# Gated linear attention with a depthwise convolution on 8 cores: two convolution taps per product on shifted copies of 64 channels, in two column tiles

## The chip, the cores and the metric

The kernel runs on all 8 cores of one Trainium2 chip, one launch for all. Each batch (4 of them) belongs to two cores: the even core computes the first 2560 tokens of the 4096, the odd core runs the state over these (without any output) and computes the other 1536. The metric is the device time of the slowest core, in microseconds. Names of engines: TensorE is PE, VectorE is DVE, ScalarE is ACT, GpSimd is POOL, SyncE is SP (here it only issues DMAs and waits).

## The reference

For each batch of 4096 tokens with 1024 features:

- layer norm, then `mixed = x W_qkv^T` (3072 channels), a causal depthwise convolution over time with 4 taps for each channel, and silu: `c[ch, t] = silu(sum over k of w[ch, k] * mixed[ch, t - 3 + k])`. The result is split into q, k and v with 16 heads of 64.
- `z = x W_z^T`, a gate `beta = sigmoid(x W_b^T)` and a decay `g = -exp(A_log) * softplus(x W_a^T + dt_bias)` for each head and token.
- q and k are normalised over the head; the state `S = S * exp(g) + k (beta v)^T` runs over the tokens, `o = q S`.
- `o` is normalised over the head, multiplied by silu(z), multiplied by W_out and added to x.
- layer norm, a product with a 1024 x 1024 matrix that is unfolded from small tensor-train factors, plus bias, added to the input of this norm.

## The kernel before, in words

**Tiles and steps.** Tokens go in tiles of 512 (`TT`), and a tile in four chunks of 128 (`NCH`). Channels go in blocks of 128 (`cc`): 0 to 7 are q, 8 to 15 k, 16 to 23 v, 24 to 31 z. An even core has 5 own tiles (`NPRE` 0, `NOWN` 5), an odd core 5 tiles that it only runs the state over (`NPRE` 5; 16 blocks, k and v, with 4 in each step) and 3 own tiles (24 blocks with convolution and 8 of z; the steps have 7, 7, 7 and 3 blocks, and the last one the z blocks too). The main loop (L1050) is software pipelined: in one step, attention works on chunk `g` of tile `t`, projection and convolution on a part of tile `t + 1`, the output product on chunk `n - 1` and the last product (`ffn`) on chunk `n - 2`. The order of instructions on every engine is the order in which this program issues them; `Lane.need` puts a wait in front, `Lane.mark` an increment behind, and every engine runs its own queue in order.

**Projection (`proj`, L508).** A block is 8 products of 128 x 128 weights and 128 x 512 columns (`proj_mm`, L503) into one of three PSUM banks (`pR`, given in turn by `ring`, L456, which waits for the release of the bank). The result is moved to `pre[:, j, 3:515]` as bf16, behind three columns that the tile before left (`halo_in` and `halo_out`, L474 and L484): by DVE for even `j` (L530), by ACT for odd `j` (L527). All blocks of a step are projected first (`fe`), then all are convolved (`fc`), with pieces of the attention between.

**Convolution (`conv`, L545).** Four products (L550), one for each tap: the stationary operand is a diagonal 128 x 128 matrix with that tap's weights, the moving operand is `pre[:, j, tap:tap + 512]`. Silu on ACT moves the sum out (L556). For k, ACT squares it too (L563), and `k2_flush` sums the squares by small products.

**Diagonal blocks (`d_issue`, L375).** In the first use of a block DVE builds the four diagonals (L386) from an identity and the taps, `d_keep` (L392) stores them in DRAM (`dscr`), and every later use loads them from there (L383). Both DMAs go through the SP queue, whose order is: wait, issue, wait, issue; a store of `dscr` in this queue waits for the build, a load waits for the convolution that frees its buffer and for the store. `ND` = 6 buffers are in turn, so a block is asked for six convolutions ahead. Weights of the projection go the same way: first use by a casting DMA from the input on the POOL queue (L366), a store to `wscr` (L373) and later loads (L363) on the SP queue.

**Attention.** `tvk` transposes v and k (TensorE) and scales them (DVE, L723 and L728); `decay` gives the decay matrix (TensorE, exp on ACT L752, cut to the triangle by POOL L756); `qk` multiplies scores by it (DVE L777); `oT` (L794) gives the output chunk in products of 64 columns with `tile_position` (0, 64 par) (L807) and (64 par, 64 par) (L813); `state` updates the state; `gate_out`, `outproj` and `ffn` follow in later steps. The norms are DVE instructions (L431, L935) and their transposes are DMAs on the SP queue (L449, L939). POOL also does q squared (L791), the bias (L945), the state's decay (L839) and its cast (L875).

**Unfolding.** In the first tiles, DVE builds the matrix of the last product in 72 pieces, some behind every projection (`uf`, L1003; 3 pieces on even cores, 1 on odd ones).

Of the kernel before, what the change touches and what calls it, by code (L numbers as in the profile page):

```python
# [5 lines left out]
F32 = mybir.dt.float32  # L6
# [9 lines left out]
NW, ND, NP, NK = 5, 6, 7, 4  # L16


def host_prep(inputs):
# [14 lines left out]
    cw = np.ascontiguousarray(  # L34
        conv_w[:, 0, :].reshape(24, 128, 4).transpose(1, 0, 2).reshape(128, 96))
# [36 lines left out]
    def t2(G2):  # L72
# [76 lines left out]
def build_program():  # L149
# [30 lines left out]
    dscr = dint("dscr", [24, 128, 512], BF16)  # L180
# [21 lines left out]
    ln2 = sb("s_ln2", [128, D])  # L202
    ln2T = [sb(f"s_ln2T{i}", [128, 8, 128]) for i in range(2)]
# [34 lines left out]
    i128b = sb("s_i128b", [128, 128])  # L238
    biasb = sb("s_biasb", [128, 1024])
# [41 lines left out]
    def emit(NPRE, NOWN):
# [44 lines left out]
        t_wab, t_i128f, t_cw, t_prow, t_bones32, t_i128b = (q_c[i].tok for i in range(6))  # L326
# [891 lines left out]
```

How the kernel before makes its waits and increments, by code:

```python
    def mark(self, ins):  # L110
        ins.then_inc(self.h, 1)
        self.v += 1
        return (self, self.v)
# [1 line left out]
    def need(self, *toks):  # L115
        for tok in toks:
            if tok is None:
                continue
            src, val = tok
            if val <= 0 or self.seen.get(src.name, 0) >= val:
                continue
            self.e.wait_ge(src.h, val)
            self.seen[src.name] = val
# [10 lines left out]
    def go(self, lane, out, in_):  # L134
        lane.e.dma_start(out=out, in_=in_).then_inc(self.h, 16)
        self.v += 16
        return (self, self.v)
# [1 line left out]
    def gotr(self, lane, out, in_):  # L139
        lane.e.dma_start_transpose(out=out, in_=in_).then_inc(self.h, 16)
        self.v += 16
        return (self, self.v)
# [122 lines left out]
    def begin(eng, name, out, in_):  # L265
        eng.dma_start(out=out, in_=in_).then_inc(sem(name), 16)
        begun.add(name)
```

## Time and profile before

| | us |
|---|---|
| median of three runs (lowest, highest) | 892.13 (885.72, 893.48) |
| the profiled execution | 892.11 |
| its span, first to last instruction of the slowest core (core 2) | 890.2 |
| spans of the eight cores | 879.7 to 890.2 |

| engine, core 2 | busy us | share of the span |
|---|---|---|
| TensorE, products | 686.3 | 77% |
| DVE | 487.2 | 55% |
| ACT | 296.8 | 33% |
| POOL | 266.9 | 30% |

The profile is one execution. Even cores and odd cores run different programs, and the slowest of all sets the time, so both kinds are to be read. A share of busy time is an average over parts with different bounds. Ends of products are modelled, so that the pitch from start to start is the safer measure of TensorE. Where a line says "x8", it is a run of instructions merged in order of time.

### The profile page before, as it was taken

The numbers are of one execution on the slowest core, as the hardware profiler recorded it, in microseconds if no ns is written. First come the engines' busy times: TensorE is split into PE (matmuls) and PEld (weight loads), VectorE is DVE, ScalarE is ACT, GpSimd is POOL, SyncE is SP. The second block draws the span as 40 slices with busy tenths as digits, with TensorE's granted clock in tenths as the row PEclk, the third lists the DMA queues.
The fourth block names the chain that finished last, engine by engine and source line by source line (L and its number), as shares of the span: only waits on it lengthen the run. The fifth ranks groups of instructions, "written<-read, shape, count | busy, mean of one in ns | idle before, by whom it ended". The sixth has DMA issues, their size and how long they took to land.

```text
span 890.2 us, 14242 instructions; the slowest of 8 cores (879.7 to 890.2 us)
## 1 busy us (share of the span) xinstructions
PE 686.3 (77%) x4687; PEld 316.4 (36%) x4767; DVE 487.2 (55%) x678; ACT 296.8 (33%) x522; POOL 266.9 (30%) x317
## 2 busy tenths in 40 slices
PE   0768674689887979979897997897999897665543
PEld 0323231234343424434343443443444443332211
DVE  4537784245656365666546657633465453656532
ACT  1143340246434325433434444413543343111100
POOL 2122111033324150450514315325044152334410
PEclk9998896799998989999899999989999999766668
DMA  9598986876366663744746456365374464122222
GB/s 195 118 238 168 182 198 184 200 205 188 78 181 171 156 175 100 203 129 152 193 132 193 122 176 168 105 169 136 116 190 105 106 163 109 41 77 67 84 59 63
DMA packets 102223, 129.00 MB, mean 145 GB/s; under 512 B 48382, under 2 KB 65284, under 8 KB 102016
## 3 DMA queue, kind: packets, MB, share of 16 engines
q1 hardware_dynamic: 88272, 99.38, 39.2%
q0 software_dynamic: 13872, 28.63, 16.7%
q8 instruction: 42, 0.69, 0.3%
q14 instruction: 37, 0.30, 0.1%
HBM read 107.40 MB, written 22.76 MB: 146 GB/s over the span
## 4 chain that ended last, share of the span: by engine, by line
PE 53%; DMA 20%; DVE 11%; issue 7%; ACT 4%; SPq 2%; POOL 2%; DVEq 0%; ACTq 0%; POOLq 0%
PE pR L503 20%; PE pR L550 9%; PE pB L912 9%; PE pA L953 7%; DMA dscr<-s_d 6%; DMA s_w<-wscr 5%; DMA wscr<-s_w 3%; DMA s_rb<-rscr 3%; DVE s_ln L935 2%; SPq L140 1%; DMA s_i128b<-i 1%; PE pB L807 1%; DMA rscr<-s_r 1%; PE pB L813 1%; DVE s_ktil L728 1%
## 5 line engine op out<-in xcount | busy, mean ns | idle before, releaser
L503 PE MATMUL pR<-s_lnxT,s_w 128*128 128x512 bf16 x1240 | 314.7, 405 | 73.2 <-DMA s_w<-wscr 27.3
L503 PEld LDWEIGHTS pR<-s_lnxT,s_w 128*128 128x128 bf16 x1280 | 126.9, 102 | 239.7 <-issue 115.7
L550 PE MATMUL pR<-s_pre,s_d 128*128 128x512 bf16 x460 | 117.1, 386 | 15.7 <-DVE s_pre L530 9.3
L135 POOL DMA_DIRECT2D rscr<-s_r x40 | 22.2, 558 | 267.4 <-ACT s_r L884 92.1
L912 PE MATMUL pB<-s_wout,s_gated 128*128 128x512 bf16 x308 | 80.7, 416 | 23.5 <-DVE s_og L826 11.6
L556 ACT ACTIVATE s_post<-pR 128x512 bf16<-128x512 f32 x120 | 68.9, 593 | 64.1 <-PE pR L550 63.6
L530 DVE CAST s_pre<-pR 128x512 bf16<-128x512 f32 x70 | 48.0, 688 | 70.1 <-PE pR L503 70.1
L918 DVE TENSOR_TENSOR s_x<-pB,s_x 128x1024 f32<-128x1024 f32 x20 | 24.5, 1225 | 101.2 <-PE pB L912 101.2
L953 PE MATMUL pA<-s_wbig,s_ln2T 128*128 128x512 bf16 x312 | 73.2, 384 | 6.6 <-DMA s_ln2T<-s_ln 6.1
L550 PEld LDWEIGHTS pR<-s_pre,s_d 128*128 128x128 bf16 x480 | 41.6, 98 | 64.5 <-issue 19.7
L527 ACT CAST s_pre<-pR 128x512 bf16<-128x512 f32 x50 | 29.3, 585 | 96.2 <-PE pR L503 96.1
L573 ACT ACTIVATE s_zT<-pR 128x512 bf16<-128x512 f32 x40 | 23.7, 597 | 110.2 <-PE pR L503 100.3
L912 PEld LDWEIGHTS pB<-s_wout,s_gated 128*128 128x128 bf16 x320 | 33.2, 106 | 66.9 <-issue 36.8
L875 POOL CAST s_Sb<-s_S 128x512 bf16<-128x512 f32 x20 | 12.2, 608 | 146.3 <-DVE s_ssb L870 146.3
L556 ACT ACT_TABLE_LOAD x20 | 25.7, 1283 | 77.6 <-PE pR L550 77.6
L756 POOL TENSOR_SCALAR_AFFINE_SELECT s_dsb<-s_dsb 128x1024 bf16<-128x1024 bf16 x40 | 44.4, 1110 | 23.6 <-ACT s_dsb L752 23.1
L414 ACT ACT_TABLE_LOAD x21 | 26.9, 1283 | 71.1 <-DVE s_pre L480 58.5
L135 POOL DMA_DIRECT2D s_w<-wcat x31 | 17.2, 557 | 101.0 <-DMA wscr<-s_w 38.8
L953 PEld LDWEIGHTS pA<-s_wbig,s_ln2T 128*128 128x128 bf16 x320 | 31.3, 99 | 44.6 <-issue 8.3
L958 DVE TENSOR_TENSOR s_x<-pA,s_x 128x1024 f32<-128x1024 f32 x20 | 24.5, 1225 | 41.1 <-PE pA L953 41.1
L945 POOL TENSOR_TENSOR s_x<-s_x,s_biasb 128x1024 f32<-128x1024 f32 x20 | 42.6, 2129 | 14.2 <-DVE s_ln L935 14.2
L897 DVE TENSOR_TENSOR s_gated<-s_og,s_rb 128x1024 bf16<-128x1024 bf16 x20 | 25.0, 1250 | 29.5 <-DMA s_rb<-rscr 29.5
(118 smaller groups left out, 891.7 us busy)
## 6 DMA issues: line engine op xcount, KB each, us to landing
s_w<-wscr SPq DMA_DIRECT2D x128, 256.0 KB, 4.6
s_d<-dscr SPq DMA_DIRECT2D x96, 128.0 KB, 3.4
s_x<-x SPq DMA_DIRECT2D x22, 512.0 KB, 5.7
s_rb<-rscr POOLq DMA_DIRECT2D x40, 256.0 KB, 4.7
y<-s_x SPq DMA_DIRECT2D x20, 512.0 KB, 2.9
s_xa<-x SPq DMA_DIRECT2D x18, 512.0 KB, 6.4
s_w<-wcat POOLq DMA_DIRECT2D x32, 256.0 KB, 6.2
wscr<-s_w SPq DMA_DIRECT2D x32, 256.0 KB, 5.6
```

Of the source, the lines that this page charges most:

```text
L135: lane.e.dma_start(out=out, in_=in_).then_inc(self.h, 16)
L414: t = S.mark(S.e.activation(out=bn[:, 14:15], in_=bn[:, 13:14], func=AF.Ln, bias=EPS5))
L503: ins = P.e.matmul(ps, w[:, dc * 128:(dc + 1) * 128], lnxT[u % 2][:, dc, :], start=(dc == 0), stop=(dc == 7))
L527: te = S.mark(S.e.copy(out=pre[:, j, 3:515], in_=ps))
L530: te = V.mark(V.e.tensor_copy(out=pre[:, j, 3:515], in_=ps))
L550: ins = P.e.matmul(ps, dr[i % ND][:, tap * 128:(tap + 1) * 128], pre[:, j, tap:tap + 512], start=(tap == 0), stop=(tap == 3))
L556: silu_tok[(u, cc)] = ring_free[k] = S.mark(S.e.activation(out=post[u % 2][:, cc, :], in_=ps, func=AF.Silu))
L756: exp_tok[(n, h2)] = G.mark(G.e.affine_select(out=d3, in_=d3, pattern=[[0, 8], [1, 128]], compare_op=ALU.is_ge, fill=zero_reg, base=0, cha ...
L897: gat_tok[n] = V.mark(V.e.tensor_tensor(out=gated.rearrange("p (a b) -> p a b", a=8), in0=og.rearrange("p (a b) -> p a b", a=8), in1=rb, o ...
L912: ins = P.e.matmul(pB[:, hf * 512:(hf + 1) * 512], gated[:, cc * 128:(cc + 1) * 128], wout[:, cc, hf * 512:(hf + 1) * 512], start=(cc == 0 ...
L945: xb_tok[n] = G.mark(G.e.tensor_tensor(out=x2[n % 3], in0=x2[n % 3], in1=biasb, op=ALU.add))
L953: ins = P.e.matmul(pA[:, hf * 512:(hf + 1) * 512], ln2T[n % 2][:, dg, :], wbig[:, dg, hf * 512:(hf + 1) * 512], start=(dg == 0), stop=(dg ...
```

## The change

The 128 channels of a block are treated as two strips of 64. `pre` gets two strips for each block: partitions 0 to 63 hold the strip's projection as before (columns 3 to 514 behind the halo), partitions 64 to 127 hold the same 64 channels shifted by one column (4 to 515). A product then has 128 rows of contraction and gives two taps at once: the stationary operand is 128 x 64, two diagonals of 64 one above the other. A block takes two passes for each of two strips, so four products of 64 columns; strip 0 goes to columns 0 to 63 of the array and PSUM partitions 0 to 63, strip 1 to columns 64 to 127 and PSUM partitions 64 to 127, in alternation.

The evacuation of a projected block is four instructions instead of one: ACT copies PSUM partitions 0 to 63 twice (to both halves of strip 0), DVE copies PSUM partitions 64 to 127 to the shifted half of strip 1 and then, inside SBUF, that to its unshifted half. The bank is free after ACT's second and DVE's first copy; the convolution waits for ACT's second and DVE's second. The halo is copied by two instructions each way.

The diagonal blocks (128 x 4 x 64) are built by GpSimd for every use, seven convolutions ahead; `dscr`, its stores and its loads are gone. To make room, the second norm shares its buffer with the first (`ln_buf`), `ln2T` has one buffer instead of two, and the squares of k have three instead of four.

The diff, cut to its core:

```diff
-NW, ND, NP, NK = 5, 6, 7, 4
+NW, ND, NP, NK = 5, 7, 7, 3
...
-    cw = np.ascontiguousarray(
-        conv_w[:, 0, :].reshape(24, 128, 4).transpose(1, 0, 2).reshape(128, 96))
+    taps = conv_w[:, 0, :].reshape(24, 2, 64, 4)
+    cw = np.zeros((128, 24, 2, 2), np.float32)
+    for ps_ in range(2):
+        cw[0:64, :, :, ps_] = taps[:, :, :, 3 - 2 * ps_].transpose(2, 0, 1)
+        cw[64:128, :, :, ps_] = taps[:, :, :, 2 - 2 * ps_].transpose(2, 0, 1)
...
-    dr = [sb(f"s_d{i}", [128, 512]) for i in range(ND)]
+    dr = [sb(f"s_d{i}", [128, 4, 64]) for i in range(ND)]
-    pre = sb("s_pre", [128, NP, 516])
-    halo = sb("s_halo", [128, 24, 4])
+    pre = sb("s_pre", [128, NP, 2, 516])
+    halo = sb("s_halo", [128, 24, 2, 4])
-    ln2 = sb("s_ln2", [128, D])
-    ln2T = [sb(f"s_ln2T{i}", [128, 8, 128]) for i in range(2)]
+    ln2T = sb("s_ln2T", [128, 8, 128])
...
         def d_issue(i):
...
-            if cc in dscr_tok:
-                Y.need(prev, q_ds[sl].tok, dscr_tok[cc])
-                d_tok[i] = q_d[sl].go(Y, dr[sl], dscr[cc])
-            else:
-                V.need(prev, q_ds[sl].tok, t_i128f, t_cw)
-                d_tok[i] = V.mark(V.e.tensor_tensor(
-                    out=dr[sl].rearrange("p (a b) -> p a b", a=4),
-                    in0=i128f[:, None, :].broadcast_to([128, 4, 128]),
-                    in1=cw[:, cc, :, None].broadcast_to([128, 4, 128]), op=ALU.mult))
-                dscr_tok[cc] = None
+            G.need(conv_tok[d_uses[i - ND]] if i >= ND else None, t_i64f, t_cw)
+            d_tok[i] = G.mark(G.e.tensor_tensor(
+                out=dr[i % ND], in0=i64f[:, None, :].broadcast_to([128, 4, 64]),
+                in1=cw[:, cc, :, None].broadcast_to([128, 4, 64]), op=ALU.mult))
...
         def halo_in(u, E):
...
-                halo_tok[u] = V.mark(V.e.tensor_copy(out=pre[:, 0:k, 0:3],
-                                                     in_=halo[:, p0:p0 + k, 0:3]))
+                V.e.tensor_copy(out=pre[0:64, 0:k, :, 0:3], in_=halo[0:64, p0:p0 + k, :, 0:3])
+                halo_tok[u] = V.mark(V.e.tensor_copy(
+                    out=pre[64:128, 0:k, :, 1:4], in_=halo[64:128, p0:p0 + k, :, 0:3]))
...
         def proj(u, cc, j):
...
-            if j % 2 == 1:
-                S.need(t, conv_tok[old] if old else None)
-                te = S.mark(S.e.copy(out=pre[:, j, 3:515], in_=ps))
-            else:
-                V.need(t)
-                te = V.mark(V.e.tensor_copy(out=pre[:, j, 3:515], in_=ps))
-            ring_free[k] = evac_tok[(u, cc)] = te
+            S.need(t, conv_tok[old] if old else None)
+            S.e.copy(out=pre[0:64, j, 0, 3:515], in_=ps[0:64, :])
+            ts = S.mark(S.e.copy(out=pre[64:128, j, 0, 4:516], in_=ps[0:64, :]))
+            V.need(t)
+            t1_ = V.mark(V.e.tensor_copy(out=pre[64:128, j, 1, 4:516], in_=ps[64:128, :]))
+            V.need(t1_)
+            tv_ = V.mark(V.e.tensor_copy(out=pre[0:64, j, 1, 3:515],
+                                         in_=pre[64:128, j, 1, 4:516]))
+            ring_free[k] = [ts, t1_]
+            evac_tok[(u, cc)] = (ts, tv_)
...
         def conv(u, cc, j):
...
-            P.need(evac_tok[(u, cc)], halo_tok[u], d_tok[i])
+            P.need(*evac_tok[(u, cc)], halo_tok[u], d_tok[i])
             k, ps = ring()
-            for tap in range(4):
-                ins = P.e.matmul(ps, dr[i % ND][:, tap * 128:(tap + 1) * 128],
-                                 pre[:, j, tap:tap + 512], start=(tap == 0), stop=(tap == 3))
+            for ps_ in range(2):
+                for st in range(2):
+                    off = 3 - 2 * ps_
+                    ins = P.e.matmul(ps[64 * st:64 * st + 64, :], dr[i % ND][:, 2 * st + ps_, :],
+                                     pre[:, j, st, off:off + 512], start=(ps_ == 0),
+                                     stop=(ps_ == 1), tile_position=(0, 64 * st))
             t = conv_tok[(u, cc)] = P.mark(ins)
-            d_keep(i)
             d_issue(i + ND)
...
         def ln2_norm(n):
             bn = bnB[n % 2]
-            V.need(l2rs_tok[n], l2_tok.get(n - 1))
+            lk = ln_buf()
+            V.need(l2rs_tok[n], ln_user[lk])
...
-            Y.need(t, ffn_tok.get(n - 2))
-            l2_tok[n] = q_tr2[n % 2].gotr(Y, ln2T[n % 2], ln2)
+            Y.need(t, ffn_tok.get(n - 1))
+            l2_tok[n] = ln_user[lk] = q_tr[lk].gotr(Y, ln2T, lnx[lk])
```

## Rows read from the trace of the kernel before

**Rows 1.** The cores, each with its span and its mean granted TensorE clock.

```profile
core 2: 890.2 us, clock 0.908
core 5: 887.3 us, clock 0.901
```

**Rows 2.** Busy us (x instructions) by engine, granted clock, DMA share, GB/s, core 2, by stretch.

```profile
27.00:167.00 140.00, 93.59 (x415) 37.22 (x419) 80.98 (x151) 40.87 (x70) 24.31 (x44) 0.88 0.83 181
167.00:747.00 580.00, 513.29 (x3683) 239.85 (x3750) 324.95 (x427) 231.93 (x403) 187.47 (x210) 0.96 0.56 152
```

**Rows 3.** Groups by shape, core 2: xcount, busy us, mean ns, idle before with its releasers.

```profile
L550 PE MATMUL pR<-s_pre,s_d 128*128 128x512 bf16 x460 | 117.1, 386 | 15.7 <-DVE s_pre L530 9.3 <-DVE s_d L386 3.2 <-issue 2.5
L530 DVE CAST s_pre<-pR 128x512 bf16<-128x512 f32 x70 | 48.0, 688 | 70.1 <-PE pR L503 70.1
L527 ACT CAST s_pre<-pR 128x512 bf16<-128x512 f32 x50 | 29.3, 585 | 96.2 <-PE pR L503 96.1
L386 DVE TENSOR_TENSOR s_d<-s_i128f,s_cw 128x512 bf16<-128x512 f32 x24 | 15.4, 687 | 20.8 <-DMA dscr<-s_d 20.7
L990 DVE CAST s_wbig<-s_x 128x512 bf16<-128x512 f32 x4 | 1.7, 427 | 0.4
```

**Rows 4.** Timeline of core 2, first tile: start us, us, engine, line, what [idle before].

```profile
94.00 0.69 DVE L386 TENSOR_TENSOR s_d<-s_i128f,s_cw 128x512 bf16<-128x512 f32 x1 [4.03 <-DMA dscr<-s_d]
96.97 3.57 PE L503 MATMUL pR<-s_lnxT,s_w 128*128 128x512 bf16 x8 [4.87 <-DVE s_pre L530]
...
148.45 0.53 POOL L135 DMA_DIRECT2D s_w<-wcat  x1 [17.73 <-DMA wscr<-s_w]
```

**Rows 5.** Timeline of core 2, attention products and convolution in a step.

```profile
368.02 0.41 PE L807 MATMUL pB<-s_dsb,s_vtok 128*64 128x128 bf16 x8
368.36 0.41 PE L813 MATMUL pB<-s_eb,s_Sb 64*64 64x128 bf16 x8
371.25 1.91 PE L550 MATMUL pR<-s_pre,s_d 128*128 128x512 bf16 x8
```

**Rows 6.** Busy time of the second step of an own tile, core 2.

```profile
350.20:380.80 30.60, 30.07 (x226) 14.46 (x229) 21.45 (x26) 13.17 (x23) 10.72 (x11) 1.00 0.64 178
```

**Rows 7.** Timeline of core 2, a first step and a second step of a tile.

```profile
327.19 3.57 PE L503 MATMUL pR<-s_lnxT,s_w 128*128 128x512 bf16 x8 [3.77 <-DMA s_w<-wscr]
...
357.99 3.61 DVE L431 TENSOR_SCALAR s_lnx<-s_xa,s_bnA 128x1024 bf16<-128x1024 f32 x1
358.07 1.11 POOL L756 TENSOR_SCALAR_AFFINE_SELECT s_dsb<-s_dsb 128x1024 bf16<-128x1024 bf16 x1
359.14 1.90 POOL L791 TENSOR_TENSOR s_qsq<-s_post 128x1024 bf16<-128x1024 bf16 x1
362.24 1.11 POOL L756 TENSOR_SCALAR_AFFINE_SELECT s_dsb<-s_dsb 128x1024 bf16<-128x1024 bf16 x1
363.31 2.13 POOL L945 TENSOR_TENSOR s_x<-s_x,s_biasb 128x1024 f32<-128x1024 f32 x1
365.40 1.04 POOL L839 TENSOR_TENSOR s_S<-s_S,s_gam 128x512 f32<-128x512 f32 x1
367.52 1.21 DVE L777 TENSOR_TENSOR s_dsb<-pA,s_dsb 128x1024 bf16<-128x1024 f32 x1
```

**Rows 8.** Single lines, core 2: min/median/max ns, first and last start, forms.

```profile
L486 DVE COPY s_halo<-s_pre x20: 167/180/2930, 46.4 to 719.0; 128x21 bf16<-128x21 bf16 x15, 128x9 bf16<-128x9 bf16 x5
L431 DVE TENSOR_SCALAR s_lnx<-s_xa,s_bnA x18: 791/1926/4245, 8.8 to 575.4; 128x1024 bf16<-128x1024 f32 x18
L788 DVE TENSOR_TENSOR s_eb<-s_post,s_eb x20: 678/684/2376, 176.0 to 829.2; 128x1024 bf16<-128x1024 bf16 x20
```

**Rows 9.** Busy time by stretch, core 1 (odd): one tile of 16 blocks, then 350 to 480.

```profile
229.90:284.00 54.10, 49.39 (x360) 24.03 (x355) 37.35 (x69) 31.92 (x53) 5.22 (x6) 1.00 0.73 189
350.00:480.00 130.00, 102.97 (x652) 46.26 (x651) 50.29 (x91) 46.03 (x77) 25.42 (x37) 0.91 0.70 164
```

**Rows 10.** Timeline of core 1 where a tile begins.

```profile
229.33 0.63 PE L587 MATMUL pG<-s_lnxT,s_wab 128*32 128x128 bf16 x32 [0.66 <-DMA s_lnxT<-s_lnx]
```

More of the change, by code:

```diff
@@ L81, in host_prep @@
         i128=np.eye(128, dtype=np.float32),
+        i64=np.tile(np.eye(64, dtype=np.float32), (2, 1)),
         ind48=np.tile(ind16, (3, 1)),
@@ L325, in emit @@
             xa_tok[m] = q_xa[m].tok
-        t_wab, t_i128f, t_cw, t_prow, t_bones32, t_i128b = (q_c[i].tok for i in range(6))
+        (t_wab, t_i128f, t_cw, t_prow, t_bones32, t_i128b,
+         t_i64f) = (q_c[i].tok for i in range(7))
         t_sel = cload(Y, sel, d_sel)
@@ L429, in ln1_norm @@
             bn = bnA[m % 2]
-            V.need(rs_tok[m], tr_tok.get(m - 2))
+            lk = ln_buf()
+            V.need(rs_tok[m], ln_user[lk])
             norm_tok[m] = V.mark(V.e.tensor_scalar(
-                out=lnx[m % 2], in0=xbuf(m), scalar1=bn[:, 12:13], scalar2=bn[:, 15:16],
+                out=lnx[lk], in0=xbuf(m), scalar1=bn[:, 12:13], scalar2=bn[:, 15:16],
                 op0=ALU.subtract, op1=ALU.mult))
@@ L479, in halo_in @@
                 V.need(halo_saved[0])
-                halo_tok[u] = V.mark(V.e.tensor_copy(out=pre[:, 0:k, 0:3],
-                                                     in_=halo[:, p0:p0 + k, 0:3]))
+                V.e.tensor_copy(out=pre[0:64, 0:k, :, 0:3], in_=halo[0:64, p0:p0 + k, :, 0:3])
+                halo_tok[u] = V.mark(V.e.tensor_copy(
+                    out=pre[64:128, 0:k, :, 1:4], in_=halo[64:128, p0:p0 + k, :, 0:3]))
         def halo_out(u, E):
             p0, k = spos(u, E[0]), len(E)
-            V.need(*[evac_tok[(u, cc)] for cc in E[-2:]], halo_tok[u])
-            halo_saved[0] = V.mark(V.e.tensor_copy(out=halo[:, p0:p0 + k, 0:3],
-                                                   in_=pre[:, 0:k, 512:515]))
+            V.need(*[x for cc in E for x in evac_tok[(u, cc)]], halo_tok[u])
+            V.e.tensor_copy(out=halo[0:64, p0:p0 + k, :, 0:3], in_=pre[0:64, 0:k, :, 512:515])
+            halo_saved[0] = V.mark(V.e.tensor_copy(
+                out=halo[64:128, p0:p0 + k, :, 0:3], in_=pre[64:128, 0:k, :, 513:516]))
         silu_tok, ksq_tok, k2_tok, z_tok = {}, {}, {}, {}
@@ L516, in proj @@
                 V.need(P.mark(ins))
-                ring_free[k] = halo_tok[u] = V.mark(V.e.tensor_copy(out=pre[:, j, 0:3],
-                                                                   in_=ps[:, 1:4]))
+                for st in range(2):
+                    r_ = slice(64 * st, 64 * st + 64)
+                    V.e.tensor_copy(out=pre[0:64, j, st, 0:3], in_=ps[r_, 1:4])
+                    halo_tok[u] = V.mark(V.e.tensor_copy(out=pre[64:128, j, st, 1:4],
+                                                         in_=ps[r_, 1:4]))
+                ring_free[k] = [halo_tok[u]]
             i, k, ps, t = proj_mm(u, cc)
@@ L572, in zproj @@
             S.need(t, og_tok.get(4 * (u - 1 - NPRE) + 3))
-            z_tok[(u, cc)] = ring_free[k] = S.mark(S.e.activation(
-                out=zT[:, cc - 24, :], in_=ps, func=AF.Silu))
+            z_tok[(u, cc)] = S.mark(S.e.activation(out=zT[:, cc - 24, :], in_=ps, func=AF.Silu))
+            ring_free[k] = [z_tok[(u, cc)]]
         gtok = {}
@@ L933, in ln2_norm @@
             bn = bnB[n % 2]
-            V.need(l2rs_tok[n], l2_tok.get(n - 1))
+            lk = ln_buf()
+            V.need(l2rs_tok[n], ln_user[lk])
             t = norm2_tok[n] = V.mark(V.e.tensor_scalar(
-                out=ln2, in0=x2[n % 3], scalar1=bn[:, 12:13], scalar2=bn[:, 15:16],
+                out=lnx[lk], in0=x2[n % 3], scalar1=bn[:, 12:13], scalar2=bn[:, 15:16],
                 op0=ALU.subtract, op1=ALU.mult))
-            Y.need(t, ffn_tok.get(n - 2))
-            l2_tok[n] = q_tr2[n % 2].gotr(Y, ln2T[n % 2], ln2)
+            Y.need(t, ffn_tok.get(n - 1))
+            l2_tok[n] = ln_user[lk] = q_tr[lk].gotr(Y, ln2T, lnx[lk])
         xb_tok = {}
@@ L952, in ffn @@
                 for hf in range(2):
-                    ins = P.e.matmul(pA[:, hf * 512:(hf + 1) * 512], ln2T[n % 2][:, dg, :],
+                    ins = P.e.matmul(pA[:, hf * 512:(hf + 1) * 512], ln2T[:, dg, :],
                                      wbig[:, dg, hf * 512:(hf + 1) * 512],
@@ L1181, in emit @@
                         out=lhalo, in_=lnxT[(NPRE - 1) % 2][:, :, 508:512]))
-        for q in (q_w + q_wc + q_ws + q_d + q_ds + q_xa + q_x2 + q_tr + q_tr2 + q_y + q_c + q_b3 + q_eb
+        for q in (q_w + q_wc + q_ws + q_xa + q_x2 + q_tr + q_y + q_c + q_b3 + q_eb
                   + q_rb + q_e + q_r + [q_a, q_i]):
```

41 lines of the change are left out of this document (23 added, 18 removed).

## The prediction, made before the change was run

> **What bounds the kernel now.** I read the spans of the cores first, then the busy time by stage, then the groups by shape, then the timelines of a few stretches. The slowest core is core 2, one of the even ones; the slowest odd core, core 5, ends 2.9 us earlier [rows 1]. Even cores run five tiles with all 24 channel blocks each, odd ones five tiles with 16 and three with 24, so both kinds have to be worked out. On core 2 the span has three parts: the first tile (27 to 167 us), with TensorE busy 94 of 140 us and the DMA engines 83%; four tiles in which attention and projections interleave (167 to 747 us), with TensorE busy 513 of 580 us [rows 2]; and the 143 us behind, a tail without convolutions. TensorE bounds the middle; DVE is at 56% there. The tail keeps its work and its waits.
>
> **The change part by part.**
>
> Products. A block has four convolution products of 512 columns. Eight of them take 1.91 us, one alone 0.386, so the pitch is (1.91 - 0.386)/7 = 0.218 us [rows 3, 5] and a block costs 0.87 us. Now there are again four, each on 64 columns of the array, in alternating column tiles. The attention has products of that form: eight with 128 moving columns start and are followed by the next kind 0.34 us later, 43 ns each with one change of tile form in it [rows 5], while 218/4 = 54 ns would be needed one after another. So the two column tiles overlap, and I price a block at half, 0.44 us. The other end is no overlap, 0.87 us. Saved on TensorE: 0.44 x 24 = 10.5 us in each full tile, 52 us on core 2. Eight overlapping at 27 ns would take 0.22 us, so a change of form costs at most 0.13 us; a step of an own tile gets about one more (outproj and ffn are now neighbours of another form, oT and state of the same): 16 x 0.13 = 2 us, which I leave in the error.
>
> Evacuation. Before, a block was moved out of PSUM by one instruction, DVE at 0.688 us (70 times) or ACT at 0.585 us (50 times) [rows 3]. Now each block takes two ACT copies (1.17 us) and on DVE one PSUM copy (0.688) and one copy SBUF to SBUF that waits for it. The trace has no bf16 copy of this size; the nearest is the 512-element cast inside SBUF at 0.427 us [rows 3], which I take as 0.43; the ends are 0.17 us (a 21-element copy, [rows 8]) and 0.69 us. ACT: 190 more at 0.585 = 111 us on top of 297, less than half the span. DVE: 120 x 1.12 = 134 us instead of 48.0. So DVE gets 86 us more here and loses 15.4 with the diagonal blocks [rows 3]. In the middle stage it goes from 325 to 325 + 96 x 1.12 - 56 x 0.69 = 394 of 580 us. That is not a bound by the share, but it sits in the projection phase of a step.
>
> Diagonal blocks. Off DVE: 24 builds. On GpSimd: 120 builds of 256 elements; an f32 product of 512 elements takes 1.04 there [rows 7], so 0.5 to 1.04 us, I take 0.55: 66 us on 267. Each waits for a convolution on TensorE and is made seven blocks ahead, a whole step, so no convolution waits for it. Queued behind it on GpSimd are the next build, the state's cast and DMA issues for the next step; none is wanted before that step, so I price it at nothing; without this cover it would be 0.55 us a block. Off the SP queue go 96 loads and 24 stores with their waits. Sharing the norm buffers, the single ln2T and three ksq buffers cost nothing: what they wait for ended one step before, or one product before the ACT instruction in front.
>
> First tile. DVE waited 20.8 us in front of its builds, nearly all for the store of an earlier one [rows 3]. One case: the build of 94.00 came 4.03 us late, the evacuation behind it too, and TensorE stood 4.87 us [rows 4]. Later the stores of weights stood behind diagonal traffic on SP, and GpSimd waited 17.73 us for one before it could ask for the next weights [rows 4]. DVE loses 15.4 + 20.8 = 36 us and gets 24 x 1.12 - 14 x 0.69 = 17 us: 19 less. The DMA engines lose 24 stores and 7 loads of 0.13 MB, 4.1 MB of 181 GB/s x 140 us = 25 MB: 22 us if they bound alone. DVE (19) and DMA (22) are both near; I take 17, and 5 to 28 as ends. A weight takes its time however early it is asked for.
>
> The step of an own tile, in which the gain is at stake. Take the second step of a tile, 30.6 us long [rows 6], and count from its start at 350.2. DVE has by then the sums and statistics of the step before to do and is free at about 2.9. Before, DVE ended the second product of scores and decay (L777) at 368.73, so at 18.5 [rows 7]; the attention's oT waits for it. Now DVE has before that point: halo 0.65, seven blocks at 1.12 (7.8), vtok and ktil 2.4 (of L777's length, 1.2), two norms at 0.8 and qtil at 0.68 [rows 8], two score products 2.4 = 15.5, so it ends at 18.4, as before. The three convolutions in front of oT gain nothing; the four behind it gain 4 x 0.44 = 1.8 us.
>
> But DVE doesn't get through undisturbed. A norm of 0.8 us took 3.61 us, from 357.99 to 361.60, while GpSimd ran from 358.07 to 361.04 without a gap [rows 7]; the 21-element copy inside SBUF took up to 2.93 us against 0.17, and the norm of the first line has a median of 1.93 against 0.79 [rows 8]. The f32 and bf16 copies out of PSUM show nothing of this. The Trainium skill, SBUF — State Buffer, section "Who interferes with whom", says why: GpSimd and a DVE copy or tensor_scalar in a two-port mode exclude each other for a whole instruction. The trace agrees by the two cases above. The new copy is one inside SBUF like L486, seven times a step. In this step GpSimd has stretches of 3.0 us (358.07 to 361.04) and 4.2 us (362.24 to 366.44) [rows 7]. The first held a norm already and will hold a copy in its place, with the norm still to come; I take 2.5 us. The second held nothing large; it comes about 1.5 us later, because ACT reaches the decay's exponentials behind more copies, and then holds the norm for most of its length, 3.4 us. DVE ends L777 at 18.4 + 5.9 = 24.3, and with the 1.8 us behind it the step is 4.1 us longer. In the first and third steps TensorE waits for a weight load (3.77 us, [rows 7]) whose issue on SP stands behind a norm. This wait covers the same delay, so there the seven blocks give 7 x 0.44 = 3.1 us back; in the third the gates' work comes in front of the norm and takes, as I estimate, 1.9 of it: -3.1 and -1.2. The last step has three blocks and eight z, whose products cover little: one held copy, +1. Tile: -3.1 + 4.1 - 1.2 + 1 = +0.8, times four = +3. Ends: -8 a tile (nearly all of 10.5 reaches the end) and +14 (three steps like the second).
>
> Odd cores. In the tiles with 16 blocks DVE is busy 37.35 of 54.1 us [rows 9]; 16 x 1.12 - 8 x 0.69 = 12.4 more makes 49.8, so the saved product time (16 x 0.44 = 7) finds DVE in the way. At the end of a tile TensorE already waits 0.66 us for the transposed norm [rows 10], which stands behind the blocks on DVE, now about 2 us later. I add 4 us for each of four tiles, +16 (0 to 30). The first tile gains 15, the tile in which the q and z weights come first (350 to 480 us, TensorE busy 103 of 130, [rows 9]) gains 12, for the same stores. The two tiles after that: +1.
>
> Sum. Even: 890.2 - 17 + 3 = 876. Odd: 887.3 - 15 - 12 + 16 + 1 = 877. The profiled execution took 892.11 us for its span of 890.2, 1.9 more, and the median of the runs is 892.13, so no correction: 878 and 879, and the slowest of eight a little above: **880 us**.
>
> **The rivals.**
> - GpSimd decides (slower). If a GpSimd stretch holds DVE in the second step's way in the first three steps of each own tile, it costs 12 x 4.1 = 49, plus 4 for the last steps, less 17: 892 + 36 = 928; halfway to the forecast, 904. It decides where the held DVE time exceeds TensorE's wait for weights, 3.8 us a step. For it: [rows 7, 8]. Against: where TensorE waits anyway it costs nothing.
> - The whole gain arrives (faster). DVE and ACT keep up, 8 us a tile and 20 at the start: 892 - 32 - 20 = 840. For it: DVE at 56%. Against: the sum of DVE's list up to L777.
> - The products don't overlap: the change does not do what it says. TensorE saves nothing, DVE's list remains, the start gains 10 less: 892 - 7 + 4 x 3 = 897, with 3 a tile for the held copies that no shorter product pays for. Against: 43 ns [rows 5].
>
> **How the numbers follow.** Forecast 0.45, its own range 865 to 895; GpSimd 0.27; whole gain 0.18; no overlap 0.10. The range reaches to 855 and to 915, which leaves out about two thirds of the whole gain's case and a third of GpSimd's, 0.2 together. A measurement of this kernel can tell about 1% (8.9 us) from no change: faster means below 883. Forecast gives 0.27 faster, 0.14 same, 0.04 slower; GpSimd 0.04 same, 0.23 slower; whole gain 0.18 faster; no overlap 0.07 same, 0.03 slower. Sum: 0.45, 0.25, 0.30.
>
> **What would show it.** The convolution's products at a pitch of about 0.11 us (half of 0.218); the SBUF copy at 0.43 us alone and at 2 us and more beside GpSimd; DVE busy near 560 us on core 2; the first tile ended near 150 instead of 167; the interval of four own tiles near 580 us still, with TensorE's idle time in front of L777's reader up. The forecast is wrong if the SBUF copy is never held, or held at each step, or if the first tile stays at 167.

## The result, and the profile after

The changed kernel takes 935.33 us (median of 4 runs, 932.31 to 938.81), beside it the kernel before 888.92: ratio 1.052, 95% interval 1.045 to 1.060. It is slower by 46 us; 880 was forecast. The profiled execution took 932.31 us. All spans grew, those of the odd cores most: to 913.6 to 918.0 us on even cores, 918.7 to 930.7 on odd ones. (Some executions of a program on eight cores are disturbed; the ratios leave these out, and where too few are left none is given.) TensorE's granted clock fell from about 0.91 to 0.86 (compare [rows 1]).

```profile
core 2: 913.6 us, clock 0.873
core 5: 930.7 us, clock 0.855
```

Both kernels compute the gates with TensorE once at the start of every tile (L587 before, L606 after). From start to start, in us, the last interval to the end of the span:

| | first starts | tiles |
|---|---|---|
| core 2 before | 26.9 | 140.1, 141.1, 149.7, 146.8, 285.7 |
| core 2 after | 30.2 | 126.5, 144.6, 157.0, 157.0, 298.4 |
| core 5 before | 33.9 | 84.6, 57.0, 53.6, 61.1, 56.1, 120.7, 135.0, 285.4 |
| core 5 after | 32.7 | 74.3, 66.9, 65.6, 78.5, 65.8, 114.3, 136.2, 296.4 |

The first tile is shorter on both, as forecast. On core 2 every tile behind it is longer; on core 5 it is the four tiles of 16 blocks behind the first (+49) and the last own one. The tail is not: from the start of its last projections to the end core 2 has 148.9 us before, 149.8 after.

Groups by shape on core 2 after, columns as in [rows 3]:

```profile
L544 DVE COPY s_pre<-s_pre 64x512 bf16<-64x512 bf16 x120 | 90.4, 754 | 12.7 <-DVE s_pre L542 0.5
L568 PE MATMUL pR<-s_pre,s_d 128*64 128x512 bf16 x480 | 82.8, 445 | 37.0 <-DVE s_pre L542 21.7 <-DVE s_pre L544 8.5 <-DVE s_wbig L1016 4.4
L388 POOL TENSOR_TENSOR s_d<-s_i64f,s_cw 128x256 bf16<-128x256 f32 x120 | 75.7, 648 | 101.7 <-PE pR L568 101.3
```

The convolution's wait for evacuation rose from 9 us to 30. DVE's two copies by single lines (min/median/max):

```profile
L542 DVE CAST s_pre<-pR x120: 687/694/696, 35.8 to 736.7; 64x512 bf16<-64x512 f32 x120
L544 DVE COPY s_pre<-s_pre x120: 291/294/4455, 36.6 to 737.5; 64x512 bf16<-64x512 bf16 x120
```

The copy from PSUM costs as much for 64 partitions as it did for 128 (0.69 us) and is never longer. Half of the copies inside SBUF take 0.29 us, the longest 4.46. The second step of an own tile shows where a long one falls (it answers to [rows 7]):

```profile
512.88 1.11 POOL L775 TENSOR_SCALAR_AFFINE_SELECT s_dsb<-s_dsb 128x1024 bf16<-128x1024 bf16 x1
513.94 2.13 POOL L965 TENSOR_TENSOR s_x<-s_x,s_biasb 128x1024 f32<-128x1024 f32 x1
516.03 1.03 POOL L858 TENSOR_TENSOR s_S<-s_S,s_gam 128x512 f32<-128x512 f32 x1
...
513.59 4.04 DVE L544 COPY s_pre<-s_pre 64x512 bf16<-64x512 bf16 x1
...
518.50 0.62 PE L568 MATMUL pR<-s_pre,s_d 128*64 128x512 bf16 x4 [2.96 <-DVE s_pre L542]
...
522.05 0.64 PE L826 MATMUL pB<-s_dsb,s_vtok 128*64 128x128 bf16 x8 [1.80 <-DVE s_dsb L796]
```

The copy stood until GpSimd's stretch was over; the last two evacuations and the scores behind it on DVE came late, and TensorE waited 2.96 us for the one and 1.80 us for the other.

In the odd cores' tiles GpSimd has little. Busy time of core 5 in one of them, before and after (columns as in [rows 2]):

```profile
175.50:229.00 53.50, 49.98 (x387) 24.39 (x387) 36.27 (x67) 31.93 (x53) 4.05 (x4) 1.00 0.64 174
```

```profile
174.00:239.70 65.70, 52.00 (x396) 24.70 (x400) 52.28 (x99) 45.41 (x78) 15.87 (x20) 0.84 0.42 111
```

DVE had 36 us of work in a tile and has 52; the tile grew by 12. TensorE's waits there (us in all, times, longest; 175 to 346 us):

```profile
PE pG L606 <- DMA s_lnxT<-s_lnx: 18.1, 2, 15.3
PE pR L568 <- DVE s_pre L542: 15.0, 15, 1.6
```

Before, the same two waits were 9.9 us (3 times, the longest 8.2) and 1.0 us (2 times). The longest one, 15.3 us, is not DVE's: it ends the tile of 78.5 us, and the transposing DMA that it waits for was asked for 1 us behind the load of W_out (2 MB, once in the kernel) and landed 1 us behind it. Of the issues between 290 and 320 us (KB each, us to landing):

```profile
s_wout<-woutd POOLq DMA_DIRECT2D x1, 2048.0 KB, 13.7
s_lnxT<-s_lnx SPq DMA_TRANSPOSE x1, 13.7
```

The median of these transposing DMAs is 3.1 us. Before, one took 10.7 us beside the same load, in the tile of 61.1 us. So 7 of the 49 us on core 5 are this wait, 15.3 instead of 8.2. That the load delays the transposing DMA is read from their coincidence; no run moves the load alone.

### The profile page after: what moved, and what is told of

Its sections match the earlier page's. It is cut to its first block, busy times and chain, and to the rows that moved or that the text cites. A ratio compares the mean times of both kernels' runs of the same rounds, so it can differ in the third digit from the quotient of the medians.

```text
span 930.7 us, 15691 instructions; the slowest of 8 cores (913.6 to 930.7 us)
## 1 busy us (share of the span) xinstructions
PE 669.8 (72%) x4872; PEld 304.7 (33%) x4872; DVE 596.1 (64%) x997; ACT 473.8 (51%) x813; POOL 293.0 (31%) x383
## 4 chain that ended last, share of the span: by engine, by line
PE 42%; DVE 22%; issue 13%; DMA 12%; ACT 7%; POOL 2%; SPq 2%; DVEq 1%; ACTq 0%; POOLq 0%
PE pR L510 21%; PE pB L931 6%; DVE s_pre L542 5%; PE pA L973 4%; PE pR L568 4%; DMA wscr<-s_w 4%; DMA s_rb<-rscr 3%; DMA s_lnxT<-s_lnx 3%; DVE s_ktil L747 2%; DVE s_lnx L433 2%; DVE s_pre L544 2%; ACT s_post L574 2%; DVE s_dsb L796 1%; PE pA L733 1%; DVE s_vtok L742 1%
## 5 line engine op out<-in xcount | busy, mean ns | idle before, releaser
L510 PE MATMUL pR<-s_lnxT,s_w 128*128 128x512 bf16 x1408 | 357.5, 410 | 27.0 <-DMA s_w<-wcat 11.6
L388 POOL TENSOR_TENSOR s_d<-s_i64f,s_cw 128x256 bf16<-128x256 f32 x152 | 99.5, 667 | 278.9 <-PE pR L568 277.0
L568 PE MATMUL pR<-s_pre,s_d 128*64 128x512 bf16 x608 | 102.2, 431 | 57.3 <-DVE s_pre L542 31.6
L539 ACT CAST s_pre<-pR 64x512 bf16<-64x512 f32 x152 | 88.0, 579 | 98.7 <-PE pR L510 98.2
L542 DVE CAST s_pre<-pR 64x512 bf16<-64x512 f32 x152 | 105.6, 695 | 33.1 <-PE pR L510 29.4
L544 DVE COPY s_pre<-s_pre 64x512 bf16<-64x512 bf16 x152 | 79.0, 520 | 15.6
L540 ACT CAST s_pre<-pR 64x512 bf16<-64x512 f32 x152 | 87.7, 577 | 1.8
L568 PEld LDWEIGHTS pR<-s_pre,s_d 128*64 128x64 bf16 x608 | 27.1, 114 | 108.2 <-issue 102.6
L142 POOL DMA_DIRECT2D rscr<-s_r x24 | 13.7, 575 | 119.0 <-ACT s_r L903 99.5
L973 PE MATMUL pA<-s_wbig,s_ln2T 128*128 128x512 bf16 x192 | 46.2, 396 | 5.9 <-DMA s_ln2T<-s_lnx 5.9
L742 DVE TENSOR_TENSOR s_vtok<-pA,s_ekT 128x1024 bf16<-128x1024 bf16 x32 | 39.2, 1224 | 8.3 <-PE pA L733 7.4
L592 ACT ACTIVATE s_zT<-pR 128x512 bf16<-128x512 f32 x24 | 14.3, 597 | 58.8 <-PE pR L510 56.6
L582 ACT ACTIVATE s_ksq<-s_post 128x512 bf16<-128x512 bf16 x64 | 40.3, 630 | 7.7 <-PE pG L554 0.4
```

Source lines behind the costliest of these rows:

```text
L388: d_tok[i] = G.mark(G.e.tensor_tensor(out=dr[i % ND], in0=i64f[:, None, :].broadcast_to([128, 4, 64]), in1=cw[:, cc, :, None].broadcast_to ...
L510: ins = P.e.matmul(ps, w[:, dc * 128:(dc + 1) * 128], lnxT[u % 2][:, dc, :], start=(dc == 0), stop=(dc == 7))
L539: S.e.copy(out=pre[0:64, j, 0, 3:515], in_=ps[0:64, :])
L540: ts = S.mark(S.e.copy(out=pre[64:128, j, 0, 4:516], in_=ps[0:64, :]))
L542: t1_ = V.mark(V.e.tensor_copy(out=pre[64:128, j, 1, 4:516], in_=ps[64:128, :]))
L544: tv_ = V.mark(V.e.tensor_copy(out=pre[0:64, j, 1, 3:515], in_=pre[64:128, j, 1, 4:516]))
```

## The experiments

The kernel before ran beside each (medians 889.96 to 892.25 us). "Even" and "odd" are spans of the cores in the profiled execution; the changed kernel has 914 to 918 and 919 to 931, the kernel before 880 to 890 on all.

**One part at a time.** Kernel before, builds by GpSimd:

```diff
-            if cc in dscr_tok:
-                Y.need(prev, q_ds[sl].tok, dscr_tok[cc])
-                d_tok[i] = q_d[sl].go(Y, dr[sl], dscr[cc])
...
+            G.need(prev, t_i128f, t_cw)
+            d_tok[i] = G.mark(G.e.tensor_tensor(
```

> The kernel before, with one part of the change alone: the diagonal blocks (128 x 512 here) are built by GpSimd for every use, without the DRAM copy, its stores and its loads. Theory D (the builds and the missing DMAs do the good of the change, at the start): the first tile of an even core gets shorter by 8 to 14 us, the later tiles stay, about 880 us. Rival (GpSimd's builds hold DVE's norms and SBUF copies, and so do the harm of the change): own tiles get longer by 3 us and more, 895 us or more.

880.11 us, ratio 0.988 (0.982 to 0.995). Even 872 to 880, odd 850 to 856. Theory D holds: core 2's first tile 125.7 us instead of 140.1, though it starts 6.6 us later; its four following unchanged within 3; core 5's first tile 84.6 to 67.2, the tile with the new q and z weights 120.7 to 112.7.

Changed kernel, products alone:

```diff
-            S.e.copy(out=pre[0:64, j, 0, 3:515], in_=ps[0:64, :])
...
+            if j % 2 == 1:
+                ts = S.mark(S.e.copy(out=pre[:, j, 0, 3:515], in_=ps))
+            else:
+                ts = V.mark(V.e.tensor_copy(out=pre[:, j, 0, 3:515], in_=ps))
```

> The changed kernel with one evacuation instruction a block as before (DVE for even j, ACT for odd j, 128 partitions, into the unshifted strip 0); both strips' products read it, so that the shifted copies are left out of the computation. Products in two column tiles and builds by GpSimd stay. Theory A (DVE's longer list, held copies included, is the whole loss): TensorE's 8 to 10 us a tile arrive, 835 to 860 us. Theory C (the products themselves cost: tile forms, a lower clock from shorter products): 880 us or more, and the granted clock of the own tiles near 0.91 as in the changed kernel instead of 0.96.

855.86 us, ratio 0.963 (0.957 to 0.969); even 844 to 854, odd 844 to 849. The products are as good as they look: 24 us less than with the builds alone. Theory C falls; the clock granted in core 2's own tiles is 0.95 (0.96 with the builds alone). (This kernel has the shared norm buffer, the single ln2T and three ksq buffers too.)

Changed kernel, evacuation alone:

```diff
-            for ps_ in range(2):
-                for st in range(2):
...
+            for tap in range(4):
+                ins = P.e.matmul(ps, dr[i % ND].rearrange("p a b -> p (a b)")[:, ...], pre[:, j, tap % 2, ...])
```

> The changed kernel with products as long as before: four products of 128 columns of the array in place of four of 64 in two column tiles, on the same copies (the weights are not those of the convolution, the time is what is looked at). The evacuation of four instructions and the builds by GpSimd stay. Theory A: DVE bounds the tiles, so 0.44 us more a block is partly hidden: 940 to 965 us. If TensorE still bounded the tiles: 10 us more in each of five tiles, 985 us.

929.26 us, ratio 1.046 (1.038 to 1.055): below both forecasts, no slower than the changed kernel, and its mean clock is 0.90 to 0.92. So behind the four evacuation instructions the halved products are worth nothing. The lower clock of the changed kernel is not the cause of the time either: core 2's three own tiles from 157 us on take 460.8 us here at a granted clock of 0.94, and 458.5 there at 0.91.

Changed kernel, diagonal blocks stored as before:

```diff
-            G.need(conv_tok[d_uses[i - ND]] if i >= ND else None, t_i64f, t_cw)
+            if cc in dscr_tok:
+                d_tok[i] = q_d[sl].go(Y, dr[sl].rearrange("p a b -> p (a b)"), dscr[cc])
```

> The changed kernel with the diagonal blocks handled as before: DVE builds each once (128 x 256), it is stored in DRAM and loaded for later uses through the SP queue. Theory D (the builds by GpSimd are good here too, because stores and loads go): about 945 us, the first tile 10 us longer. Rival (GpSimd's 0.6 us builds hold DVE's copies, so that they carry a part of the loss): 920 us or less.

946.53 us, ratio 1.063 (1.061 to 1.066): 11 us above the changed kernel, as theory D has it. The builds are a gain with either evacuation.

**DVE's second copy.** Left out:

```diff
-            tv_ = V.mark(V.e.tensor_copy(out=pre[0:64, j, 1, 3:515],
-                                         in_=pre[64:128, j, 1, 4:516]))
+            tv_ = t1_
```

> The changed kernel without DVE's second copy (the one inside SBUF, 0.29 us unheld, 0.75 mean on core 2, 0.52 on core 5); strip 1's products read strip 0. DVE still copies PSUM once a block. Theory B (the held SBUF copies decide): even cores lose nearly all of their loss and come to 885 to 892, odd cores, where GpSimd has little, gain only some 10 us. Theory A (the sum of DVE's list decides): both kinds gain about what DVE saves in the tiles at the unheld price and a part of the holds, since these fall on the next norm: 905 to 915 us on either kind.

906.75 us, ratio 1.020 (1.012 to 1.028). Even 878 to 880 (38 us less), odd 894 to 903 (27 less). Theory B for even cores, which gain even more than it said; on odd ones 27 is more than the 10 us that B allowed and nearer to A. On core 5 the four tiles of 16 blocks behind the first are 16 us shorter, 8 of them by the wait beside the load of W_out (7.2 instead of 15.3); the three tiles with 24 blocks are 17 us shorter.

From PSUM instead of SBUF:

```diff
-            V.need(t1_)
-            tv_ = V.mark(V.e.tensor_copy(out=pre[0:64, j, 1, 3:515],
-                                         in_=pre[64:128, j, 1, 4:516]))
-            ring_free[k] = [ts, t1_]
+            tv_ = V.mark(V.e.tensor_copy(out=pre[0:64, j, 1, 3:515], in_=ps[64:128, :]))
+            ring_free[k] = [ts, tv_]
```

> The changed kernel with DVE's second copy reading PSUM again (0.69 us, a kind that no trace shows held) instead of SBUF (0.29 unheld; means of 0.75 on core 2 and 0.52 on core 5). Theory A (the sum of DVE's list decides): even cores, where 0.69 and the mean of 0.75 are near to each other, stay at 915 to 920; odd cores get 64 to 152 copies longer by 0.17 to 0.4 us, 935 to 950. Theory B (it is the long single holds that hurt, since they fall in the way of the attention): even cores come down by 10 us and more although the sum stays.

922.25 us, ratio 1.037 (1.032 to 1.042). Even 888 to 899, 25 us less, though this copy has nearly the same mean (core 2):

```profile
L543 DVE CAST s_pre<-pR 64x512 bf16<-64x512 f32 x120 | 83.5, 696 | 3.7
```

Here 120 copies of 0.70 replace 120 of 0.75: the sum on DVE is the same, single long ones are gone. That is theory B. Odd: 909 to 923, some 8 us less than the changed kernel, where theory A wanted 935 to 950. DVE's copies are 27 us more on core 5 (105.7 instead of 79.0), so the sum of DVE's list does not decide there either. In the four tiles of 16 blocks core 5 is 3 us longer (7 more at three of them, 4 less at the one with the load of W_out); from its last own tile to the end it is 11 us shorter.

On ACT:

```diff
-            V.need(t1_)
-            tv_ = V.mark(V.e.tensor_copy(out=pre[0:64, j, 1, 3:515],
-                                         in_=pre[64:128, j, 1, 4:516]))
+            S.need(t1_)
+            tv_ = S.mark(S.e.copy(out=pre[0:64, j, 1, 3:515], in_=pre[64:128, j, 1, 4:516]))
```

> The changed kernel with the copy inside SBUF made by ACT, which then has three copies a block and waits for DVE's copy in front of the third; DVE keeps one. DVE's list is that of the kernel without this copy (906.8 us, even cores 879, odd 899). Theory A with ACT (51% busy) free enough: 905 to 915 us. Rival (ACT's longer list and its wait for DVE take the place): 920 us or more.

940.91 us, ratio 1.058 (1.056 to 1.060). Even 918 to 922. DVE has the list of the 906.8 us kernel, so ACT's third copy, waiting in ACT's queue for DVE, gives all of it back. Whether by its length or by its wait this run does not separate. ACT's second copy left out instead:

> The changed kernel without ACT's second copy (strip 0's shifted half; its products read strip 1), DVE's two copies stay. Theory A and B (DVE is in the way, not ACT): within 5 us of the changed kernel, 930 to 940 us, and if less, by ACT's later exponentials only. Rival (ACT's 120 to 152 more copies are a part of the loss): 15 us less and more, 920 us or below.

942.58 us, no ratio; the lowest execution, 930.0, is all that can be compared, 2 us below the lowest of the changed kernel. That fits theories A and B, not the rival's 920.

**GpSimd's side.** Without the bias addition:

```diff
-                if on2:
-                    add_bias(n2)
```

> The changed kernel without the addition of the bias by GpSimd (left out of the result; 2.13 us of GpSimd in each of 20 steps on even cores, 12 on odd ones), nothing else changed. Theory B: the stretch of 4.2 us in a step is cut in two halves, the mean of the copy inside SBUF on core 2 falls from 0.75 to about 0.5 us and even cores gain 10 to 20 us; odd cores gain in their three own tiles alone, 3 to 6 us. Theory A (the sum of DVE's list): the same fall of DVE's busy time, but a gain under 5 us.

932.46 us, ratio 1.048 (1.045 to 1.050). Even 885 to 892 (27 less, more than theory B's 10 to 20), odd 928 to 933 (no change, where B had 3 to 6). On core 2:

```profile
L544 DVE COPY s_pre<-s_pre 64x512 bf16<-64x512 bf16 x120 | 67.3, 561 | 12.7 <-DVE s_pre L542 0.5
```

No DVE instruction was touched, and a GpSimd instruction of 2.1 us a step was worth 27 us on even cores. With it moved in front of the output product, nothing left out:

```diff
-                if on2:
-                    add_bias(n2)
...
                 fz(2)
+                if on2:
+                    add_bias(n2)
                 if on1:
                     outproj(n1)
```

> The changed kernel with the addition of the bias moved in the same way, so that nothing is left out. Theory B: as in the kernel without this addition (even cores 885 to 892, odd 928 to 933), the time stays with the odd cores, 930 us; the even cores come to 885 to 895. Rival (what is moved holds DVE elsewhere): even cores above 905.

928.34 us, ratio 1.040 (1.035 to 1.045). Even 892 to 903 (19 less), odd 919 to 930. Most of the effect on even cores is in the place.

**Order on DVE.** The first norm moved forward, behind vtok and ktil, on the kernel with builds alone:

```diff
                     tvk(g)
+                ln1_norm(m)
...
                 fe(2)
-                ln1_norm(m)
```

> The kernel before with builds by GpSimd (880.1 us) and the first norm of a step moved forward in the same way. Theory B (in own tiles it is single holds of DVE by GpSimd that cost; the norm has a mean of 2.59 us there against 0.80 alone): the norm then runs before GpSimd's stretch, its mean falls to about 1 us and the even cores gain 5 to 15 us, 865 to 875. Rival: what stands behind the norm is held instead (L788's kind of copy, the state's work), or TensorE had the wait covered: 876 to 884 us.

922.74 us, ratio 1.037 (1.031 to 1.042): 43 us slower by one line, even cores 906 to 921. The rival holds. Core 2:

```profile
484.37 4.93 DVE L774 TENSOR_TENSOR s_eb<-s_post,s_eb 128x1024 bf16<-128x1024 bf16 x1
489.22 1.28 DVE L517 CAST s_pre<-pR 128x512 bf16<-128x512 f32 x2
...
490.05 6.32 PE L490 MATMUL pR<-s_lnxT,s_w 128*128 128x512 bf16 x16 [5.68 <-DVE s_pre L517]
```

GpSimd's stretch (484.56 to 488.75 us) now holds the instruction in front of two evacuations, and TensorE stands 5.68 us for a bank. The same on the kernel with the second copy from PSUM:

> The changed kernel with the second copy from PSUM (922.3 us; even cores near 890, odd near 920), and the first norm of a step moved forward, behind vtok and ktil instead of behind the fourth projection. Theory L (on odd cores a part of the loss is the transposed norm that TensorE waits for where a tile begins, 26 us in 90 to 370 us on core 5 there, because the norm stands late in DVE's list): this wait falls to about 10 us and odd cores come to 905 to 912. Rival (DVE's list itself makes the tiles long, the wait for the norm is only where it shows): the wait moves to the convolutions, odd cores stay within 5 us of 920.

932.69 us, ratio 1.050 (1.046 to 1.053); odd 922 to 930, even 913 to 915 (21 more). Theory L falls, and the rival has the mechanism: on core 5, from 90 to 370 us, the wait for the transposed norm went from 25.9 us to nothing, and the convolutions' wait for evacuation from 47.4 to 58.8.

**Odd cores.** Unfolding as on even cores:

```diff
-        RATE = 3 if NPRE == 0 else 1
+        RATE = 3
```

> The changed kernel with the 72 pieces of the unfolding (about 0.7 us of DVE each) done by odd cores as by even ones, three behind every projection of the first tile and a half, instead of one behind every projection over five tiles. Theory A (on odd cores the length of DVE's list in a step bounds the tiles over which only the state runs): the third to fifth tile get 16 x 0.7 = 11 us shorter in DVE's list and 5 to 10 us in time (from 65.6, 78.3 and 65.8), the first gets longer by 10 to 20; odd cores 910 to 925, even cores stay at 917. Rival (these tiles wait for something else, the transposed norm or ACT): they stay within 2 us and the first tile's loss is added, 940 us.

938.49 us, ratio 1.052 (1.046 to 1.057). Core 5's tiles: 81.6, 81.8, then 61.1, 61.0, 62.8 instead of 65.6, 78.5, 65.8. The three are 25 us shorter, the first two 22 longer. But 13 of the 25 are the wait beside the load of W_out, which here was asked for behind the transposing DMA (2.6 instead of 15.3 us). What is left is 3 to 5 us a tile for about 10 us less of DVE. One of them:

```profile
194.30:255.00 60.70, 49.00 (x387) 23.46 (x387) 42.46 (x82) 45.66 (x77) 13.04 (x20) 0.92 0.50 120
```

Theory A had the direction, with less than its 5 to 10 us a tile, and its 910 to 925 for odd cores did not come; the rival's 940 did, though not by its mechanism. Both moves together:

> The changed kernel with both moves, the bias and the unfolding: whether the change can be made good by giving DVE room. If the two effects add: even cores 885 to 892, odd 905 to 920, so 905 to 920 us, still above the kernel with builds alone (880). If they don't: 925 us and more.

933.63 us, ratio 1.046 (1.036 to 1.056); even 890 to 896, odd 920 to 927. The change isn't made good by this.

**Two taps for every other block:**

```diff
+            if cc % 2:
+                ts = S.mark(S.e.copy(out=pre[:, q, 2, 3:515], in_=ps))
+                evac_tok[(u, cc)] = (ts, ts)
+                return
```

> Two taps per product for every other block only (even blocks: two ACT copies and two DVE copies, products in column tiles); odd blocks as before (one ACT copy, four products of 128 columns). Builds by GpSimd. DVE has per two blocks 0.98 us and its holds, against 0.69 before and 1.96 in the changed kernel. Theory A (the loss begins where DVE's list exceeds TensorE's in the projections of a step): half of the product time, 4 to 5 us a tile, comes out against the kernel with builds alone (880 us): 858 to 872 us. Theory B (single holds decide, wherever a copy inside SBUF meets GpSimd): 880 to 895.

909.57 us, ratio 1.020 (1.012 to 1.028); even 892 to 897, odd 896 to 907. Neither forecast: slower than the builds alone on both kinds. On core 5 a tile of 16 blocks takes 62.5 us with DVE busy 49.2: half of the change brings most of the longer list (41.4 with the builds alone, 52.3 in the changed kernel) and most of the longer tile.

**Towards a better version.** The kernel with builds alone and the bias moved:

> The kernel before with builds by GpSimd (880.1 us, even cores near 876, odd near 853), and GpSimd's addition of the bias (2.13 us a step) moved from the projections of a step to the place in front of the output product, where DVE has little. Theory B (what counts is what stands behind the DVE instruction that a GpSimd stretch holds): the stretch of 4.3 us in the projections is cut, the norm's mean falls from 2.59 to about 1.5 us, even cores gain 8 to 20 us: 858 to 870. Rival (the hold moves to DVE's gating product and its followers, or TensorE waits for weights there anyway): 874 to 882 us.

No ratio; the two lowest executions, 877.3 and 879.6 us, are no faster than without the move: the rival's side. The start of the kernel is another place where DVE is held. It looks like this in the changed kernel and in the one with builds alone, core 2:

```profile
17.07 4.53 POOL L388 TENSOR_TENSOR s_d<-s_i64f,s_cw 128x256 bf16<-128x256 f32 x7
17.20 3.94 DVE L433 TENSOR_SCALAR s_lnx<-s_xa,s_bnA 128x1024 bf16<-128x1024 f32 x1
```

```profile
17.90 6.55 DVE L418 TENSOR_SCALAR s_lnx<-s_xa,s_bnA 128x1024 bf16<-128x1024 f32 x1
```

```diff
+        G.need(norm_tok[3])
         for i in range(ND):
             d_issue(i)
```

> The kernel before with builds by GpSimd, whose first six wait for the last of the four first norms. In the kernel with builds alone DVE's second norm took 6.55 us beside the six builds (17.84 to 23.90), and the first tile began at 33.5 us instead of 26.9. Theory B: that norm takes 0.80 again, the first tile begins near 27.5, every core gains 5 to 6.5 us: 872 to 876. Rival (the later builds make the first convolution or DVE's following copies late): 878 us or more.

875.56 us, ratio 0.984 (0.979 to 0.988). The norm takes 0.79 us, and the first tile starts at 26.96 instead of 33.5.

> The same, with the addition of the bias moved in front of the output product too. In the first look at that move the even cores had 868 to 876 us against 872 to 880. If that was an effect: 868 to 872 us, 3 to 4 below the kernel without the move. If not: within 1 us of it.

**869.22 us, ratio 0.974 (0.969 to 0.979)**: the fastest version that computes the whole result, with the convolution as it was before. It is 6 us below the kernel without the move.

## Why the prediction was wrong

Two steps of the prediction failed. On even cores it was the step of an own tile, where waits for weights were to cover the held copies: +3 us in four tiles, measured +34. On odd cores it was the +16 for the four tiles with 16 blocks, where DVE's longer list was to make each tile 4 us longer: measured +49. The odd cores end last, so the second sets the time. Term by term:

- **Products** (0.44 us a block, pitch 0.11). Right: four take 0.62 us and eight 1.06, so four more cost 0.44. Alone they are worth 24 us (880.1 to 855.9).
- **Diagonal blocks** (GpSimd, nothing). Right in the tiles; missed at the start, where on core 2 seven builds without a gap stand beside the first norms: 3.3 us.
- **First tile** (-17 and -15). The direction is right: 13.6 less on core 2 and 10.3 on core 5; the late start takes 3.3 of the first back.
- **Length of the SBUF copy** (0.43). 0.29 alone. DVE was to gain 71 us of work on core 2 and got 110 (487 to 597): 120 x (0.754 - 0.294) = 55 of it is held time, if the median is taken as the copy's length alone.
- **The step of an own tile.** -3.1 + 4.1 - 1.2 + 1 = +0.8 a tile was said; the four tiles of core 2 grew by 3.5, 7.3, 10.2 and 12.7. The one that starts at 458 us, step by step: +0.9, +5.7, +2.1, +1.7, 10.3 in all. The second step went as described (a held copy, late scores). The gains in the first and third steps weren't there: I had them from waits for weights that would cover the delay. In the first step a held copy stood in front of ktil, and TensorE waited in the projections, ahead of any weight that was late:

```profile
466.54 3.46 DVE L544 COPY s_pre<-s_pre 64x512 bf16<-64x512 bf16 x1
...
472.53 0.94 PE L765 MATMUL pA<-s_ind,s_b 115*128 115x512 bf16 x2 [4.06 <-DVE s_ktil L747]
```

  The rival "GpSimd decides" had the mechanism; it gave +36 us, core 2 got +23. That its 928 us lies near the measured 935 is luck: it counted the even cores, and the odd ones set the time.
- **Odd cores** (+16 in four tiles). Measured +49. DVE's list is 52 of 66 us, not 49.8 of 54; I took the list as one more thing that comes 2 us late. The kernel with long products has the same tile (65.1 us), so the product time came back as waiting: 15.0 us for evacuation from 175 to 346 us, 1.0 before. 7 of the 49 are the transposing DMA beside the load of W_out, which the prediction did not look at. That the list is a cause is shown by its direction alone: about 10 us less of it gave 3 to 5 us a tile. The q/z tile gained 6.4 of 12; the two own tiles behind it cost 12, not 1.
- **What the Trainium skill says of holds** (SBUF — State Buffer, section "Who interferes with whom"). It says that GpSimd and a DVE copy in a two-port mode exclude each other. Where the copy read PSUM no hold appeared (0.70 us at most), and where it read SBUF they did (up to 4.46): the traces agree. The same section says that a DVE instruction with two SBUF inputs contends with GpSimd's reads too; L774 in the kernel with the earlier norm, held 4.93 us against a median of 0.69, agrees. It has the later of the two blocked for a whole instruction of the other; here the measured holds went on over three and more of GpSimd's instructions.

**What stays open.** With DVE at 42.5 us in a tile of 16 blocks the changed kernel takes 61 us, with 41.4 and one-instruction evacuation 55.6; what makes the rest is open, and with it the larger part of the odd cores' loss. Without ACT's second copy ACT is busy 35.8 instead of 45.4 us in such a tile on core 5, DVE 53.4, and the tile takes 64.6 us (65.5 with it), so beside DVE's long list that copy counts for little; the chain PSUM copy, SBUF copy, product was not tried alone (the kernel with the second copy from PSUM has no such chain, but 4 us more of DVE, and takes 68.3). Nor do I know why the move of the bias shows with late builds (6 us) and not without.

## What to carry to other kernels

A product that is made cheaper by preparing its operand moves work to the engines that prepare it. Add that work to each engine's list within the step where it stands, not to its share of the span, and ask what waits at the end of that list. A GpSimd stretch without a gap was a wall here for DVE's copies and norms inside SBUF, not for its copies from PSUM: look at which instruction it meets and what is queued behind that one. Before a tile that grew is put down to an engine's list, look at what its longest wait was for: here two fifths of what one tile grew by, and most of what two experiments took off it, was one wait beside a large load. When a change of several parts fails, time each part alone: here one of three was the loss, and the other two made the kernel faster.

## What the hardware showed unexpectedly

A held DVE instruction can wait through several GpSimd instructions that follow without a gap: a copy of 0.29 us took 4.04 across three of them (1.11, 2.13 and 1.03 us), a norm of 0.80 took 6.55 beside six builds (6.06 us). A transposing DMA of 3.1 us took 13.7 beside a load of 2 MB. A copy of 64 x 512 bf16 inside SBUF takes 0.29 us, one from PSUM 0.69 whether it has 64 or 128 partitions. And where this wall stands decides more than its length: moving one norm forward in a step cost 43 us, moving one GpSimd addition gave 19 on the even cores of the changed kernel and 6 in the fastest.
